# Four cross-attention layers on one core: inputs also loaded transposed, weights in seven loads, a new order table

## The reference

```
L0: x1 = LN(x + mha(x, x))           # causal; L0 a=0
    x2 = LN(x1 + mha(x1, ctx))       # a=1
    x3 = LN(x2 + fc2(relu(fc1(x2)))) # h, z
L1: rms-norm, rotary attention (16 heads over 4 key heads of 64) on ctx, plus mask1   # a=2
    x = x + o; x = x + down(silu(gate(n)) * up(n)),  n = rms-norm(x)
L2: x = x + Wo(mha(LN(x), LN(ctx)))  # a=3
L3: s = clip((q k) * (0.5 + 0.5*mask3), -50, 50); x = LN(x + Wo(softmax(s) v))        # a=4
mha of L0: rows of x that are all zero are masked; the length of the keys is the
count of nonzero entries in the first row of q k, the rest of the keys are -inf
```

## Time and profile before

| | |
|---|---|
| median of three runs | 4310.21 us (4309.85 to 4310.59) |
| the profiled execution | 4308.03 us |
| its span, first to last instruction | 4306.2 us |
| PE busy | 4007.5 us, 93%, 44768 matmul instructions |
| PE weight loads busy | 3474.5 us, beside the matmuls |
| DVE, ACT, POOL busy | 2876.9 (67%), 2731.0 (63%), 1226.6 (28%) |
| the chain that ended last | PE 50%, DVE 33%, issue 7%, POOL 6%, ACT 4% |
| DMA | 53.10 MB, queue of the loads 3.3% of the engines' time |

### The profile page before, as it was taken

One profiled execution on the slowest core, in us unless ns is written; L12 is line 12 of the kernel. 1 busy time (PEld: TensorE's weight loads), 2 busy tenths in 40 slices (PEclk: granted clock), 3 DMA queues, 4 the chain that ended last, 5 costly groups with the idle time before them and its releaser, 6 DMA issues.

```text
span 4306.2 us, 119430 instructions
## 1 busy us (share of the span) xinstructions
PE 4007.5 (93%) x44768; PEld 3474.5 (81%) x44768; DVE 2876.9 (67%) x10721; ACT 2731.0 (63%) x8513; POOL 1226.6 (28%) x2247
## 2 busy tenths in 40 slices
PE   4899999999999999999999999999999999999997
PEld 3788888888888888888888888888888888888885
DVE  3576676676676666766766766766766766766664
ACT  2566666666666666666666666666666666666663
POOL 0222322322322322323323323323223223223221
PEclk8999999999999999999999999999999999999998
DMA  3000000000000000000000000000000000000000
GB/s 126 2 12 7 11 12 7 12 12 7 11 12 7 12 11 7 11 12 7 12 11 7 11 7 12 12 7 12 12 7 12 11 7 11 12 7 12 11 3 5
DMA packets 47365, 53.10 MB, mean 12 GB/s; under 512 B 5328, under 2 KB 46288, under 8 KB 46416
## 3 DMA queue, kind: packets, MB, share of 16 engines
q1 hardware_dynamic: 46800, 45.46, 3.3%
HBM read 37.05 MB, written 8.39 MB: 11 GB/s over the span
## 4 chain that ended last, share of the span: by engine, by line
PE 50%; DVE 33%; issue 7%; POOL 6%; ACT 4%; DVEq 0%; DMA 0%; POOLq 0%; ACTq 0%
PE gen_ps L477 31%; PE gen_ps L469 7%; DVE masked L939 5%; PE scores_ps L554 4%; DVE masked L946 4%; PE gen_ps L578 3%; POOL rstd L773 3%; PE gen_ps L589 3%; DVE st L913 2%; DVE masked L949 2%; POOL prob L826 2%; DVE xs L923 1%; DVE zn L908 1%; ACT res L762 1%; PE scores_ps L533 1%
## 5 line engine op out<-in xcount | busy, mean ns | idle before, releaser
L477 PE MATMUL gen_ps<-actT,w_sb 128*128 128x128 f32 x11264 | 1423.6, 279 | 13.0 <-ACT actT L685 6.2
L477 PEld LDWEIGHTS gen_ps<-actT,w_sb 128*128 128x128 f32 x11264 | 1330.9, 193 | 126.1 <-ACT actT L685 75.6
L685 ACT ACTIVATE probT<-gen_ps 128x512 f32<-128x512 f32 x1024 | 606.7, 623 | 333.1 <-PE gen_ps L469 332.8
L773 POOL TENSOR_TENSOR rstd<-ve,consts 128x1 f32<-128x1 f32 x448 | 268.3, 599 | 1849.2 <-DVE ve L915 978.5
L718 ACT ACTIVATE prob<-scores_ps,negmax 128x128 f32<-128x128 f32 x2048 | 571.5, 415 | 197.2 <-DVE negmax L952 197.2
L469 PE MATMUL gen_ps<-consts,prob 128*128 128x128 f32 x4096 | 596.7, 277 | 20.0 <-ACT prob L718 6.2
L469 PEld LDWEIGHTS gen_ps<-consts,prob 128*128 128x128 f32 x4096 | 476.8, 142 | 84.4 <-POOL prob L826 25.7
L477 PE MATMUL gen_ps<-w_sb,actT 128*128 128x256 f32 x2048 | 539.4, 386 | 2.4 <-ACT actT L753 1.4
L685 ACT ACTIVATE actT<-gen_ps 128x256 f32<-128x256 f32 (+1 forms) x576 | 268.5, 478 | 329.1 <-PE gen_ps L469 329.1
L477 PE MATMUL gen_ps<-w_sb,wide 128*128 128x256 f32 x2048 | 463.2, 379 | 0.0
L952 DVE TENSOR_REDUCE negmax<-scores_ps 128x4 f32<-128x512 f32 x512 | 328.8, 684 | 198.7 <-ACT prob L718 114.1
(11 more groups left out here) (123 smaller groups left out, 5943.8 us busy)
## 6 DMA issues: line engine op xcount, KB each, us to landing
ctx_rms<-x_dram SPq DMA_DIRECT2D x64, 128.0 KB, 2.2
ctx<-ctx_dram SPq DMA_DIRECT2D x64, 128.0 KB, 2.2
mask<-mask_dram SPq DMA_DIRECT2D x128, 64.0 KB, 2.0
out_dram<-res SPq DMA_DIRECT2D x64, 128.0 KB, 1.7
w_sb<-weights_dram SPq DMA_DIRECT2D x1, 7680.0 KB, 23.8
w_sb<-weights_dram SPq DMA_DIRECT2D x1, 2048.0 KB, 28.2
rows_sb<-rows_dram SPq DMA_DIRECT2D x1, 1408.0 KB, 6.1
consts<-consts_dram SPq DMA_DIRECT2D x1, 460.5 KB, 3.3
```

What stands on the lines that cost most here:

```text
L477: last = nc.tensor.matmul(ps, lhsT(c), rhs(c), start=(c == 0), stop=(c == chunks - 1))
L685: release(nc.scalar.activation(dst, take(act, name, b)[:, 0:width], ACT.Copy), name, b)
L773: nc.gpsimd.tensor_tensor(dst, src, const("expo")[:, 0:width], ALU.pow)\
```

## The change

- x and ctx are given a second time, transposed by the host, and loaded into `actT` and a new tile `ctxT`: PE's `xT` step, its copy on ACT, and the two context blocks of `tr` 4 are gone; `mask3` comes transposed, so PE's `mask4` step is gone too (DVE forms its factor from the loaded mask). DVE's part of `xT` is the step `rows_in`.
- `ctx_ln` shares the buffer of `ctx_rms` and is a POOL step of its own, after `tr` 2 has read `ctx_rms`.
- The weights come in seven loads, in the order of use, between the first two batches' inputs; the setup block is gone and its work is a list of steps (`betas`, `bo`, seven `scale`) that stand once among the steps of the first batches (`ONCE`), each product waiting for its own weights.
- `once` drops a wait when the same engine has already waited for that value or a higher one; where a step lists several waits, the one expected last stands first; `BANK_LATE` puts the bank's wait of `turn` 3.2 and 3.3 ahead of the others.
- The table has a new `PERIOD` and new times, and with them another order on each engine. The lines shown are the steps that the prediction speaks of.

On PE a period now reads (batch offsets left out): attended0 queries0 turn3.0-3.3 scores2 values3 tr1 attended3 queries1 zT3 keys1 keys0 first_row1 o3 turn2.0 turn2.1 tr4 scores1 turn2.2 queries4 turn2.3 out2 out2 turn1.0 keys4 o2 turn1.1 first_row0 turn1.2 turn1.3 scores4 nT3 values1 gate0 attended1 up0 scores0 gate1 x2T values4 h up1 z attended4 down turn0.0 zT4 turn0.1 turn0.2 tr2 o4 tr3 q2.0 queries3 turn0.3 keys3 q2.1 scores3 values0 kv2.

Before it was: attended0 turn3.0-3.2 xT turn3.3 scores2 values3 tr1 queries0 attended3 queries1 keys1 mask4 keys0 zT3 turn2.0 first_row1 o3 turn2.1 scores1 turn2.2 tr4 turn2.3 out2 out2 queries4 turn1.0 keys4 turn1.1 o2 turn1.2 turn1.3 scores4 values1 nT first_row0 attended1 gate0 up0 gate1 scores0 x2T up1 h values4 z down turn0.0 attended4 turn0.1 turn0.2 zT4 tr2 tr3 o4 queries3 turn0.3 keys3 q2.0 scores3 q2.1 values0 kv2.

On DVE, of the same period: attended0 queries0 stats0 norm0 soft2.0 soft2.1 attended3 soft2.2 soft2.3 ... first_row1 prob_norm o3 prob_norm ctx_norms soft1.0 ... o2 mean_square first_row0 rms_norm3 soft4.0-4.3 attended1 gate0 stats1 norm1 soft0.0 up0 soft0.1 gate1 soft0.2 soft0.3 up1 z attended4 norm_x3 mean_square down rms_norm2 norm_x4 o4 norm4 q2.0 queries3 rows_in q2.1 soft3.0-3.3 mask4 kv2.

```diff
-PERIOD = 68.67
+PERIOD = 71.632128
...
-    ("xT", 0, 0, {"PE": 4.90, "ACT": 0.00, "DVE": 14.42}),
-    ("queries", 0, 0, {"PE": 6.89, "DVE": 23.79}),
-    ("scores", 0, 0, {"PE": 44.51}),
-    ("attended", 0, 0, {"PE": 67.18, "DVE": 80.19, "POOL": 78.71}),
-    ("tr", 1, 0, {"PE": 75.56, "ACT": 72.47}),
-    ("ctx_norms", 0, 0, {"DVE": 89.28, "POOL": 85.92}),
-    ("nT", 3, 0, {"PE": 178.11, "ACT": 172.46}),
-    ("down", 3, 0, {"PE": 183.99, "DVE": 200.82, "POOL": 178.30}),
-    ("attended", 3, 0, {"PE": 213.11, "DVE": 231.31}),
-    ("mask4", 4, 0, {"PE": 219.69, "DVE": 234.93}),
-    ("attended", 4, 0, {"PE": 253.00, "DVE": 270.14}),
...
+    ("queries", 0, 0, {"PE": 0.000, "DVE": 26.987}),
+    ("rows_in", 0, 0, {"DVE": 15.480}),
+    ("scores", 0, 0, {"PE": 42.724}),
+    ("attended", 0, 0, {"PE": 69.715, "DVE": 98.158, "POOL": 60.591}),
+    ("tr", 1, 0, {"PE": 77.619, "ACT": 86.670}),
+    ("ctx_norms", 0, 0, {"DVE": 112.468, "POOL": 79.369}),
+    ("ctx_ln", 2, 0, {"POOL": 156.335}),
+    ("nT", 3, 0, {"PE": 178.003, "ACT": 189.075}),
+    ("down", 3, 0, {"PE": 194.548, "DVE": 219.804, "POOL": 186.410}),
+    ("attended", 3, 0, {"PE": 225.494, "DVE": 243.432}),
+    ("mask4", 4, 0, {"DVE": 237.582}),
+    ("attended", 4, 0, {"PE": 265.534, "DVE": 289.233}),
...
+SCALED = [("q2", 0, 2048, "rms1"), ("kv2", 0, 1024, "rms1"), ("gate", 0, 2048, "rms2"), ("up", 0, 2048, "rms2"),
+          ("qk3", 0, 256, "gq"), ("qk3", 256, 256, "gkv"), ("v3", 0, 256, "gkv")]
+SCALED = [(w, first, min(width, W_OFF[w][1] // 2), gain) for w, first, width, gain in SCALED]
+ONCE = [
+    ("betas", 0, {"PE": 69.726, "DVE": 98.169}),
+    ("bo", 0, {"PE": 83.681, "DVE": 107.485}),
+    ("scale", 4, {"DVE": 98.202}),
+    ("scale", 5, {"DVE": 98.213}),
+    ("scale", 6, {"DVE": 98.224}),
+    ("scale", 0, {"DVE": 99.597}),
+    ("scale", 1, {"DVE": 110.191}),
+    ("scale", 2, {"DVE": 132.607}),
+    ("scale", 3, {"DVE": 134.576}),
+]
...
+LOADS = [("first", "qk0", "v0"), ("second", "qk1", "fc2"), ("third", "q2", "kv2"), ("last", "qk3", "o4"),
+         ("o2", "o2", "o2"), ("gate", "gate", "up"), ("down", "down", "down")]
...
+    events += [(times[engine], name, 0, 0, u) for name, u, times in ONCE if engine in times]
...
-        ctx_ln = sb("ctx_ln", [P, G, D])
+        ctxT = sb("ctxT", [P, G, C, P])
+        ctx_ln = ctx_rms
...
+BANK_LATE = {"t32", "t33"}
...
+        passed = {}
+        def once(eng, semaphore, value):
+            if passed.get((id(eng), id(semaphore)), 0) < value:
+                eng.wait_ge(semaphore, value)
+                passed[id(eng), id(semaphore)] = value
...
         def take(eng, name, i):
-            eng.wait_ge(bank_full[j], use)
+            once(eng, bank_full[j], use)
...
         def read_out(eng, name, i):
-            eng.wait_ge(bank_read[j], use)
+            once(eng, bank_read[j], use)
...
+        def tensor_program(pe):
+            def ready(w):
+                times = sum(w == other for other, *_ in SCALED)
+                if times:
+                    once(pe, sem(f"scaled_{w}"), times)
+                else:
+                    once(pe, sem(f"w_{load_of(w)}"), 16)
+            def betas(b):
+                pe.wait_ge(sem("w_last"), 16)
+                ps = begin("betas", b)
                 for k, (w, first, beta) in enumerate([("qk3", 0, "betaq"), ("qk3", 256, "betakv"), ("v3", 0, "betakv")]):
                     for n in range(C):
-                        for c in range(C):
-                            last = nc.tensor.matmul(gen_ps[:, 0, 2 * k + n:2 * k + n + 1],
-                                                    W(w)[:, c, first + n * P:first + (n + 1) * P], col(beta, c),
-                                                    start=(c == 0), stop=(c == C - 1))
-                last.then_inc(sem("su_beta"), 1)
-                pe.wait_ge(sem("su_vb"), 1)
+                        last = product(ps[:, 2 * k + n:2 * k + n + 1],
+                                       lambda c: W(w)[:, c, first + n * P:first + (n + 1) * P],
+                                       lambda c: col(beta, c), C)
+                end(last, "betas", b)
+            def output_biases(b):
+                pe.wait_ge(sem("vb_wide"), 4)
+                ps = begin("bo", b)
                 for a in range(2):
-                    for c in range(C):
-                        last = nc.tensor.matmul(gen_ps[:, 1, a * D:(a + 1) * D], masked[:, c, 0, :]
-                                                if a == 0 else probT[:, c, 0, :], W(f"o{3 + a}")[:, c, :],
-                                                start=(c == 0), stop=(c == C - 1))
-                last.then_inc(sem("su_bo"), 1)
...
+            def late_bank(name, b):
+                if name in BANK_LATE:
+                    begin(name, b)
...
+            def inputs_ready(a, b):
+                if a:
+                    read_out(pe, f"tr{a}", b)
+                else:
+                    once(pe, xT_sem(b), 16 * (b // G + 1))
...
             def keys(a, b):
+                late_bank(f"sv{a}", b)
+                if a == 4:
+                    once(pe, ctxT_sem(b), 16 * (b // G + 1))
+                else:
+                    inputs_ready(a, b)
+                ready(f"v{a}")
+                src = ctxT[:, g, :, :] if a == 4 else actT[:, g, 2:4, :]
...
             def scores(a, b):
+                if f"scores{a}" in BANK_LATE:
+                    scores_read(pe, a, b)
                 if a == 2:
                     pe.wait_ge(sem("roped"), 4 * (b + 1))
-                else:
+                if a < 2:
+                    pe.wait_ge(sem(f"pen_{a}"), b + 1)
+                    once(pe, sem("picked"), 1)
+                if a != 2:
                     read_out(pe, f"m{a}", b)
                     read_out(pe, f"sv{a}", b)
-                if a < 2:
-                    pe.wait_ge(sem(f"pen_{a}"), b + 1)
                 scores_read(pe, a, b)
                 for k in range(HU if a < 2 else 0):
                     for r in range(R):
...
             def values(a, b):
-                    for u in range(U):
+                    for u in reversed(range(U)):
                         read_out(pe, f"t{a}{u}", b)
...
                 elif name == "tr" and a == 1:
-                    pe.wait_ge(sem("x1"), b + 1)
                     pe.wait_ge(sem("ctx_m"), b + 1)
                     transposes("tr1", b, halves(xs[:, g, :]) + halves(ctx_m[:, g, :]))
...
                 elif name == "tr" and a == 4:
                     read_out(pe, "o3", b)
-                    transposes("tr4", b, halves(xs[:, g, :]) + halves(ctx[:, g, :]))
-                elif name == "mask4":
-                    pe.wait_ge(mask3_sem(b), 16 * (b // G + 1))
-                    transposes("mask4", b, [mask3[:, g, :]])
+                    transposes("tr4", b, halves(xs[:, g, :]))
...
+                    nc.gpsimd.tensor_scalar(ctx_rms[:, g, :], ctx[:, g, :], crstd[:, g, 1:2], 0.0,
+                                            ALU.mult, ALU.add).then_inc(sem("ctx_rms"), 1)
+                elif name == "ctx_ln":
+                    j, use = plan["tr2", b]
+                    once(pool, bank_full[j], use)
                     nc.gpsimd.tensor_scalar(ctx_ln[:, g, :], ctx[:, g, :], cmv[:, g, 0:1], crstd[:, g, 0:1],
                                             ALU.subtract, ALU.mult).then_inc(sem("ctx_ln"), 1)
-                    nc.gpsimd.tensor_scalar(ctx_rms[:, g, :], ctx[:, g, :], crstd[:, g, 1:2], 0.0,
-                                            ALU.mult, ALU.add).then_inc(sem("ctx_rms"), 1)
...
+            def biases(b):
+                ps = take(dve, "betas", b)
+                for c in range(C):
+                    nc.vector.tensor_tensor(vbias[:, 0, c:c + 1], ps[:, 4 + c:5 + c], col("bv3", c), ALU.add)
+                    nc.vector.tensor_copy(vbias[:, 1, c:c + 1], col("bv4", c)).then_inc(sem("biases"), 1)
+                    nc.vector.tensor_tensor(kbias[:, 0, c:c + 1], ps[:, 2 + c:3 + c], col("bk3", c), ALU.add)
+                    nc.vector.tensor_copy(kbias[:, 1, c:c + 1], col("bk4", c)).then_inc(sem("biases"), 1)
+                    nc.vector.tensor_copy(qbias[:, 1, c:c + 1], col("bq4", c)).then_inc(sem("biases"), 1)
+                    ins = nc.vector.tensor_tensor(qbias[:, 0, c:c + 1], ps[:, c:c + 1], col("bq3", c), ALU.add)
+                release(ins, "betas", b)
+                read_out(dve, "betas", b)
+                dve.wait_ge(sem("biases"), 6)
+                for a in range(2):
+                    for c in range(C):
+                        nc.vector.tensor_copy(vb_wide[:, a, c, :], vbias[:, a, c:c + 1].to_broadcast([P, P]))\
+                            .then_inc(sem("vb_wide"), 1)
+            def scale(u):
+                w, first, width, gain = SCALED[u]
+                dve.wait_ge(sem(f"w_{load_of(w)}"), 16)
+                if load_of(w) == "last":
+                    read_out(dve, "betas", 0)
+                for c in range(C):
```

(37 more changed lines are left out.)

347 lines of the change are left out of this document (166 added, 181 removed).

## The result

The changed kernel takes **4096.57 us** (4093.7 to 4099.65, 4 runs) where the one before took 4310.4 in the same comparison (4309.85 to 4312.23, 4 runs): a ratio of 0.9504, 95% interval 0.9489 to 0.9519. The prediction said 4229 and a range from 4145 to 4285.

What follows compares the result with a forecast made beforehand. It took TensorE, 93% busy but also held by waits, to set a 65.1 us period repeated some 60 times. Saving 0.9 us a period (54) and 27 at the start gave 4227, or 4229 on the median's scale; range 4145 to 4285.

Steps and rivals of the forecast that it cites:

- 37 - 6.5 - 3.9: Start: first product 37 us earlier, less 6.5 for setup behind batch 0's attended and 3.9 for the output-bias product: 27 us.
- (a): turn 3.3 takes the bank of queries 0, which DVE reads behind attended 0: 0.7 us with a small one before.
- (b): attended 3, right behind tr 1, waits for ACT's copy of values 3: 0.45 us, and queries 1 0.2.
- (c): tr 4, now before scores 1, waits for DVE's o 3 behind the row penalty's chain: 0.65 us.
- (d): turn 1.0 feels DVE's ctx_norms, moved to before soft 1: 0.2 us.
- (e): nT 3 waits because its rms_norm stands behind the row penalty's chain (first_row 0) on DVE: 0.5 us.
- (f): up 3.1 needs the bank of gate 3.1, which DVE reads behind soft 0.1: 0.7 us.
- (g): tr 2 waits for rms_norm 2, behind down's add and statistics, with one step less of PE work before: 0.85 us.
- (h): scores 3 behind q2 1 makes soft 3 some 2 us later on ACT: 0.5 us for attended 0 and tr 1.
- C: Rival: the new order's waits are mostly not there, 1.5 us a period less: 4139 us; chance 0.14.
- B: Rival: the period does not move, PE waits what it saves; only the start is gained: 4283 us; chance 0.14.
- D: Rival: slower, since late soft 3 delays ACT's following steps and 2 us come round each period: 4373 us; chance 0.08.

Runs made afterwards that it cites:

- x4_setup: Changed kernel with all weights loaded first and bias products, scalings and wide copies done before batch 0, as before: 4123.61 us.
- x3_cm: Changed kernel with three of five removed transposes back (two of the context, one of the mask): 4117.18 us.
- x1_waits: Changed kernel with its wait lists as before, repeated waits issued again and late waits in their old places: 4104.96 us.
- u_att4: Changed kernel with attended 4 again behind down and turn 0.0, and zT 4 behind turn 0.2: 4150.29 us.
- u_nT: Changed kernel with values 1 again ahead of nT 3 on TensorE and ScalarE: 4114.16 us.
- x2_cm: Changed kernel with the old table of steps and the context's and mask's three transposes back: 4271.06 us.
- x2_table: Changed kernel with the old table of steps, without the transposes that no longer exist: 4257.75 us.
- x5_tab: Changed kernel with setup, wait lists and three transposes (context and mask) as before; new table and loaded transposed x stay: 4151.62 us.
- u_q0b: Changed kernel with queries 0 right before tr 1 on TensorE, and read behind soft 2.1 on VectorE, as before: 4145.85 us.
- u_soft4: Changed kernel with VectorE's soft 4 steps pulled apart: 4.2 behind attended 1, 4.3 behind stats 1 and gate 3.0: 4332.37 us.
- u_q0: Changed kernel with queries 0 right before tr 1 on TensorE alone, VectorE's order unchanged: 4549.96 us.
- i_f: Changed kernel with gate 3.1 ahead of soft 0.1 on VectorE, nothing else moved: 4064.69 us.
- i_fc: i_f with tr 4 also behind scores 1 on TensorE, queries 4 left between turn 2.2 and 2.3: 4063.42 us.
- i_cfg: Changed kernel with gate 3.1 ahead of soft 0.1, tr 4 behind scores 1, queries 4 behind turn 2.3, o 4 ahead of tr 2: 4109.93 us.
- i_cfgb: i_cfg with keys 0 between tr 1 and attended 3 on TensorE, and two steps sooner on ScalarE: 4222.91 us.

## Why the prediction was wrong in size and right in direction

*The start*: right, 27 forecast, 27.0 (x4_setup) measured. That it fits so well is luck in part, for its terms erred against each other. The first product came at 9.05, not 6.9: I let the 768 KB pass at 432 GB/s, but the load was issued at 2.58 and landed 6.3 later. `rows` and the context's loads were issued while it was under way; that they slowed it is my reading, no run shows it. From `attended` 0 to `tr` 1 it is 14.5, not 13. The output-bias product takes 2.2 (49.44 to 51.66), not 3.9, and even these are not paid: against x4_setup the first product is 35.7 earlier, `tr` 1 28.7 earlier and the first store still 28.7. So of 37 - 6.5 - 3.9 the runs show 35.7 - 7.0 - 0. The Trainium skill's "DMA: Bandwidth & Descriptors", "Anatomy of one DMA", puts a fixed cost of about 2 us on a transfer issued by GpSimd; had it held here for each load in series, it would by estimate have asked for 10 us more. The loads of this kernel are issued by SP, the first product was 2.15 late, and the issues of the first three weight loads took 0.43 to 0.49 each and those of the last four 4.13 together, without a wait for a landing.

*The transposes*: right. 0.107 us each (x3_cm) for my 0.11. By the 275 ns that the Trainium skill's "TensorE: Matmul & The Clock Gate", Part 4, gives for a transpose (of bf16, in one kernel), taken as a cost each, the three would have cost an estimated 53 us; the measurement of 20.6 decides, and the granted clock is 1.00 in the steady windows with and without them.

*The lists and the small gaps*: I took 0.5 us a period for the gaps, half of 0.9, and nothing more for the lists. What is left of the 3.0 us when transposes (0.55) and waits (2.1 to 2.2) are taken off is 0.3, of which 0.13 are the lists (x1_waits). The term was 0.2 too high.

*Cost of the loads, `ctx_ln` on GpSimd, `rows_in`*: 0 was said. `rows_in` waits 1.3 us a period for its load on DVE (`absmax` L876, 76.3 us over 61 times), and no wait of PE's list points to it; right behind it VectorE still idles 0.41 for PE (`wide` L985).

*The order*: **the step that failed.** I set 4.6 us of waits that go against 4.75 that come, "each is my estimate [...] and could be off by half". The places that it names for the going side come to 4.1 (`scores` 1's 0.64 among them); 0.5 are short holds without a place. As a whole it fits: with the period at 65.13, work at 59.6 and gaps at 0.9, 4.6 are left for waits. By a run of its own only `zT` 4 was looked at, 0.71 for 0.8 and made of other parts (u_att4); u_nT does not show what `values` 1 was worth. The coming side was nearly twice too large:

| wait | forecast | measured | 
|---|---|---|
| (a) `turn` 3, with `scores` 2 | 0.7 | 0.60 |
| (b) `attended` 3, `queries` 1 | 0.65 | 0.42 |
| (c) `tr` 4, `scores` 1 | 0.65 | 0.49 |
| (d) `turn` 1.0 | 0.2 | 0 |
| (e) `nT` 3 | 0.5 | 0.09 |
| (f) `up` 3.1 | 0.7 | 0.46 |
| (g) `tr` 2 | 0.85 | 0.38 |
| (h) `attended` 0, `tr` 1 | 0.5 | 0.03 |

4.75 against 2.47: 2.3 us a period, 60 times 137 us, where the miss is 132; the term of the gaps, 0.2 a period too high, worked the other way, and the rest is the start and rounding. Five of the eight places are those of my walk, with the engines that it named; (d), (e) and (h) are all but empty, and every size is too high. I had written that each could be off by half. Half of 4.75 would have been 2.4, nearly what was measured, and a period shorter by 3.3; my range let the period gain at most 1.5. Two of the eight sizes show how. For (e) I counted the length penalty's chain of 1.4 whole in front of `rms_norm` 3. VectorE's timeline, and GpSimd's:

```profile
1734.11 0.42 DVE L1104 TENSOR_TENSOR xs<-gen_ps,xs 128x256 f32<-128x256 f32 x1 [5.24 <-PE gen_ps L467]
...
1735.18 0.34 DVE L910 TENSOR_SCALAR nz<-gen_ps,consts 128x128 f32<-128x128 f32 x1
...
1736.52 0.34 DVE L1096 TENSOR_SCALAR zn<-xs,rstd 128x256 f32<-128x256 f32 x1
```

```profile
1735.35 0.56 POOL L788 TENSOR_TENSOR rstd<-ve,consts 128x1 f32<-128x1 f32 x1 [10.05 <-DVE ve L1091]
```

`rms_norm` 3 (1736.52) needs GpSimd's root, done at 1735.91. Of the penalty's 1.34 (1735.18 to 1736.52) 0.73 lies beside that and only 0.6 is in the way; and TensorE itself is busy with `scores` 4 nearly until the norm is done at 1736.86 (`nT` 3 starts at 1736.92). For (h), ScalarE's last exponentials of `soft` 3:

```profile
1707.06 3.24 ACT L733 ACTIVATE prob<-scores_ps,negmax 128x128 f32<-128x128 f32 x12
1710.06 2.19 ACT L699 ACTIVATE probT<-gen_ps 128x512 f32<-128x512 f32 x4
```

They end at 1710.3, 2.9 us after `attended` 0, and the four copies of `turn` 3 at 1712.25, before `values` 3 begins on TensorE (1713.12). The lateness was real and 0.9 us of slack lay behind it. Both are the same error: a lateness was entered as a wait without what else ran beside it. That it explains the other six too was not shown one by one.

*Rivals.* C, my waits mostly absent, at 4139, was the nearest: half of their sum is absent, 2.3 us a period where it took 1.5. B is refuted as a whole, but what it says holds in part under the old order (x2_cm). D's mechanism does not show: `soft` 3 is done 2.9 us after `attended` 0, and nothing comes round with it.

That it is the table which carries some 145 to 161 of the 214 us is shown by x2_table, x2_cm and x5_tab. That it does so through fewer and shorter waits, 4.6 to 2.5 us a period, is read from the traces. How much each exchange carries is not shown: undoing one alone gave 43 and 47 us in the periods for two (u_att4, u_q0b), and for two others a mixture with a new wait of its own (u_nT, u_soft4).

## What to carry to other kernels

When one engine is over 90% busy and a hand-written order decides its waits, a reordering can be worth more than removed work: here 161 us against 34 for five transposes a batch. Size each new wait from the starts of rows of the trace, and enter a late step as a wait only after taking off what its reader waits for anyway. If each size could be off by half, let the range of the sum say so. A step moved on one engine has to be moved on those that read it (u_q0: 453 us; u_q0b: 49). And a hold in the trace is not yet a price: taking out `up` 3.1's gained all of it (i_f, 32 us), taking out `tr` 4's a fifth (i_fc), taking out `tr` 2's less than nothing (i_cfg), since the next late step takes its place. A number that fits is no proof either: u_nT met its forecast with another wait than the one forecast, which only the trace showed.

## What the runs showed of the hardware

A long wait on TensorE is paid twice. After each 4.5 us of idle time the granted clock was 0.50 for 3.4 to 6.2 us, 2.3 us lost on average (u_q0); after 2.9 us it was so in two of three periods, for 6.2 and 3.5 us, which cost 2.9 and 1.6 us (u_soft4). Behind waits of 0.85 us and less the windows of the steady periods show 1.00 (i_cfgb). What D's 2 us would have done lies between these and was not run; I had priced them without the clock. And wait instructions whose semaphore has long passed cost little: 59 a batch, on all engines together, came to 0.13 us.
